# Splitting the time-step products of a Mamba-style scan into two fp16 parts

## The reference

```python
z, x, B_toks, C_toks, dt_toks = split(u @ W_in.T)     # 512, 512, 64, 64, 8
x, B_toks, C_toks = silu(causal_conv4(x, B_toks, C_toks))
A  = -exp(A_log)                                      # one value per head, 8 heads
dt = softplus(dt_toks + dt_bias)
dA = exp(dt * A)
# per token and head:
S = S * dA_t + outer(dt_t * x_t, B_t);  y_t = S @ C_t
y = (y + D * x) * silu(z);  out = y @ W_out.T
```

## Time and profile before

| | |
|---|---|
| median of 3 runs (lowest, highest) | 1589.3 us (1588.49, 1592.45) |
| profiled execution: span from first to last instruction | 1590.2 us (no other time is listed for it) |
| TensorE busy / VectorE / ScalarE / GpSimd | 1431.8 / 1034.1 / 592.3 / 541.7 us |
| mean granted TensorE clock | 0.962 of full |
| first stage / second stage | about 0 to 860 us / 860 to 1590 us |

### The profile page before, as it was taken

One profiled execution on the slowest core, in us unless ns is written; L12 is line 12 of the kernel. 1 busy time (PEld: TensorE's weight loads), 2 busy tenths in 40 slices (PEclk: granted clock), 3 DMA queues, 4 the chain that ended last, 5 costly groups with the idle time before them and its releaser, 6 DMA issues. The chain is left out here.

```text
span 1590.2 us, 23447 instructions
## 1 busy us (share of the span) xinstructions
PE 1431.8 (90%) x7392; PEld 707.9 (45%) x7392; DVE 1034.1 (65%) x2288; ACT 592.3 (37%) x1046; POOL 541.7 (34%) x653
## 2 busy tenths in 40 slices
PE   3798897898979988899886999999999999999998
PEld 1354443443535434445443444444444444444443
DVE  6799797897886978969885535435363545445333
ACT  4365554654645546555453221203020221213020
POOL 1275655556465555665754001010101001010101
PEclk9899998998999999989998999999999999999999
DMA  5011122022121221112201101010100101010000
GB/s 168 1 49 49 49 62 64 15 72 59 38 63 36 62 62 49 59 39 62 62 22 59 53 9 46 1 55 1 54 1 21 34 7 47 1 53 1 27 1 27
DMA packets 37454, 65.22 MB, mean 41 GB/s; under 512 B 5056, under 2 KB 15296, under 8 KB 37312
## 3 DMA queue, kind: packets, MB, share of 16 engines
q1 hardware_dynamic: 35424, 63.47, 12.7%
q10 hardware_dynamic: 1888, 0.03, 0.1%
HBM read 46.71 MB, written 16.78 MB: 40 GB/s over the span
## 5 line engine op out<-in xcount | busy, mean ns | idle before, releaser
L1386 ACT ACTIVATE gtanh<-bank,c_gate_half 128x512 f32<-128x512 f32 (+1 forms) x88 | 60.4, 687 | 537.0 <-PE bank L1421 537.0
L1421 PE MATMUL bank<-xt,ffn_hi 128*128 128x512 f16 (+1 forms) x704 | 213.8, 386 | 13.4 <-DVEq L82 6.7
L991 DVE TENSOR_SCALAR mask<-codes_h 128x416 f16<-128x416 f16 x640 | 215.5, 368 | 1.9
L1421 PE MATMUL bank<-xt_odd,ffn_hi 128*128 128x512 f16 (+1 forms) x704 | 209.4, 379 | 0.0
L1359 POOL TENSOR_TENSOR drstd<-dvar,neg_half 128x1 f32<-128x1 f32 x32 | 17.4, 545 | 481.1 <-DVE dvar L1518 481.1
L828 PE MATMUL bank<-mask,diag 128*128 128x416 f16 x640 | 133.2, 353 | 46.8 <-DVE mask L991 46.6
L1493 DVE SCALAR_TENSOR_TENSOR gsilu<-gtanh,bank 128x512 f32<-128x512 f32 (+1 forms) x88 | 60.5, 687 | 137.6 <-ACT gtanh L1386 137.4
L1421 PE MATMUL bank<-xt,ffn_lo 128*128 128x512 f16 (+1 forms) x352 | 135.7, 385 | 0.0
L1445 PE MATMUL bank<-ffn_hi,h_hi 128*128 128x512 f16 (+1 forms) x352 | 133.5, 379 | 0.0
L1421 PE MATMUL bank<-xt_odd,ffn_lo 128*128 128x512 f16 (+1 forms) x352 | 133.4, 379 | 0.0
L1445 PE MATMUL bank<-ffn_hi,h_lo 128*128 128x512 f16 (+1 forms) x352 | 133.3, 379 | 0.0
(11 more groups left out here) (184 smaller groups left out, 2768.3 us busy)
## 6 DMA issues: line engine op xcount, KB each, us to landing
codes_sb<-codes SPq DMA_DIRECT2D x80, 208.0 KB, 3.5
ut<-u SPq DMA_DIRECT2D x8, 1024.0 KB, 5.7
ures<-u SPq DMA_DIRECT2D x32, 256.0 KB, 2.7
x_scratch<-x SPq DMA_DIRECT2D x32, 256.0 KB, 2.0
xf<-x_scratch SPq DMA_DIRECT2D x8, 1024.0 KB, 5.9
out<-res SPq DMA_DIRECT2D x32, 256.0 KB, 2.0
ffn_hi<-w_in_t SPq DMA_DIRECT2D x4, 580.0 KB, 10.3
ffn_hi<-w_out_t SPq DMA_DIRECT2D x1, 1024.0 KB, 14.5
```

What stands on the lines that cost most here:

```text
L991: ins = nc.vector.tensor_scalar(mask[:, n, q, :], codes_h[:, n, :], float(2 * q), None, ALU.is_equal)
L1386: gtanh_ready.inc(nc.scalar.activation(gtanh[0:w, m % 2, :], banks[2 + m % 2][0:w, :], ACT.Tanh, scale=c_gate_half[0:w, :]))
L1421: last = nc.tensor.matmul(bank, wt[:, c0:c0 + w], xts[i][:, half, k, :], start=(k == 0 and n == 0), stop=(k == KC - 1 and n == 2))
```

## The change

Step 17 now writes dt * A * 2^7 in fp32 (`dax`); step 18 writes its high part in fp16 into `da[..., 0, :]`, clipped from below at -2^15; step 19 writes the remainder in fp16 into `da[..., 1, :]`; dt/4 becomes step 20. POOL's `segments` multiplies both parts, 2048 columns of fp16. The zero-one matrices get fp16 copies, made once on VectorE. TensorE adds the products of both parts in PSUM: four fp16 products of 512 columns, and six of 8 columns, for the chunk. The two exponentials take the scale 2^-7. In `time_steps` all 16 masks now stand beside steps 4 to 19.

```diff
-            da = st("da", [P, 2, SUB, HEADS])
+            dax = st("dax", [P, SUB, HEADS])
+            da = st("da", [P, 2, SUB, 2, HEADS], F16)
-            seg = st("seg", [P, HEADS, P])
+            seg = st("seg", [P, 2, HEADS, P], F16)
...
                         if c == 0:
-                            pool.wait_ge(dt_steps.sem, dt_steps.now(t, 17))
+                            pool.wait_ge(dt_steps.sem, dt_steps.now(t, 19))
                         seg_ready.inc(nc.gpsimd.tensor_tensor(
-                            seg[:], causal[:].unsqueeze(1).broadcast_to((P, HEADS, P)),
-                            da[:, p, c, :].unsqueeze(2).broadcast_to((P, HEADS, P)), ALU.mult))
+                            seg[:].rearrange("p n h t -> p (n h) t"),
+                            causal_h[:].unsqueeze(1).broadcast_to((P, 2 * HEADS, P)),
+                            da[:, p, c].rearrange("p n h -> p (n h)").unsqueeze(2).broadcast_to((P, 2 * HEADS, P)),
+                            ALU.mult))
...
-                        pe.wait_ge(dt_steps.sem, dt_steps.now(t, 17))
-                        for n, sums in enumerate((causal, below, ones)):
-                            last = nc.tensor.matmul(banks[3][:, 192 + n * HEADS:192 + (n + 1) * HEADS], sums[:],
-                                                    da[:, half, c, :], start=True, stop=True)
+                        pe.wait_ge(dt_steps.sem, dt_steps.now(t, 19))
+                        for n, sums in enumerate((causal_h, below_h, ones_h)):
+                            last = split_products(banks[3][:, 192 + n * HEADS:192 + (n + 1) * HEADS],
+                                                  [(sums[:], da[:, half, c, i, :]) for i in range(2)])
...
                         for n in range(2):
-                            last = nc.tensor.matmul(banks[4 + n][:], below[:],
-                                                    seg[:, 4 * n:4 * n + 4, :].rearrange("p h t -> p (h t)"),
-                                                    start=True, stop=True)
+                            last = split_products(banks[4 + n][:], [
+                                (below_h[:], seg[:, i, 4 * n:4 * n + 4, :].rearrange("p h t -> p (h t)"))
+                                for i in range(2)])
...
                         t_step(17, nc.vector.tensor_tensor(
-                            da[:, p], dt[:], a_sb[:].unsqueeze(1).broadcast_to((P, SUB, HEADS)), ALU.mult))
-                        t_step(18, nc.vector.tensor_scalar(dt4[:, p], dt[:], 0.25, None, ALU.mult))
+                            dax[:], dt[:], a_sb[:].unsqueeze(1).broadcast_to((P, SUB, HEADS)), ALU.mult))
+                        t_step(18, nc.vector.tensor_scalar(da[:, p, :, 0, :], dax[:], DA_LEAST * DAS, None, ALU.max))
+                        t_step(19, nc.vector.scalar_tensor_tensor(
+                            da[:, p, :, 1, :], dax[:], DA_LEAST * DAS, da[:, p, :, 0, :], ALU.max, ALU.subtract))
+                        t_step(20, nc.vector.tensor_scalar(dt4[:, p], dt[:], 0.25, None, ALU.mult))
...
-                            time_steps(i, p, lambda j: one_mask(row, half, 4, j))
-                            masks(row, half, 4, first=15)
+                            time_steps(i, p, lambda j: one_mask(row, half, 4, j) if j < 2 * PAIRS else None)
...
+                    for half, full in ((causal_h, causal), (below_h, below), (ones_h, ones)):
+                        nc.vector.tensor_copy(half[:], full[:]).then_inc(s_ident, 1)
```

More of the change, by code:

```diff
@@ L68 @@
 HSCALE = 2.0 ** -54
+DAS = 2.0 ** 7
+DA_LEAST = -2.0 ** 8
 class Signal:
@@ L161, in sandwich_kernel @@
         ident_h = sb("ident_h", [P, P], F16)
+        causal_h = sb("causal_h", [P, P], F16)
+        below_h = sb("below_h", [P, P], F16)
+        ones_h = sb("ones_h", [P, P], F16)
         dve_passed, pool_passed = sem("dve_waits_passed"), sem("pool_waits_passed")
@@ L272, in sandwich_kernel @@
             xs_ready = Signal(sem("conv_silu_ready"), FB + 1)
-            dt_steps = Signal(sem("dt_steps"), 18)
+            dt_steps = Signal(sem("dt_steps"), 20)
             dt_exp = Signal(sem("dt_exponential"), 1)
@@ L432, in weights @@
                         if c == 0:
-                            pool.wait_ge(dt_steps.sem, dt_steps.now(t, 18))
+                            pool.wait_ge(dt_steps.sem, dt_steps.now(t, 20))
                         xdt_ready.inc(nc.gpsimd.tensor_tensor(
@@ L541, in _ @@
                     front_rstd(0)
+                    pool.wait_ge(s_ident, 4)
                     pool.wait_ge(s_big, KC + 3)
@@ L642, in small @@
                         sums_ready.inc(nc.scalar.activation(
-                            ex[:], banks[3][:, 192:216].rearrange("p (k h) -> p k h", k=3), ACT.Exp))
+                            ex[:], banks[3][:, 192:216].rearrange("p (k h) -> p k h", k=3), ACT.Exp, scale=1.0 / DAS))
                         sums_ready.inc(nc.scalar.activation(bt[:], banks[3][:, 128:192], ACT.Copy))
@@ L649, in decays @@
                             decay_ready.inc(nc.scalar.activation(
-                                decay[:, 4 * n:4 * n + 4, :], banks[4 + n][:].rearrange("p (h t) -> p h t", h=4), ACT.Exp))
+                                decay[:, 4 * n:4 * n + 4, :], banks[4 + n][:].rearrange("p (h t) -> p h t", h=4), ACT.Exp, scale=1.0 / DAS))
                     def y_transposed(t, c):
@@ L952, in body @@
                         decode(t, 4, more)
-                    pe.wait_ge(s_ident, 1)
+                    pe.wait_ge(s_ident, 4)
                     for s in range(SUB):
@@ L1230, in _ @@
                     dve.wait_ge(s_alog, 1)
-                    step(nc.vector.tensor_scalar(a_sb[:], a_sb[:], -1.0, None, ALU.mult))
+                    step(nc.vector.tensor_scalar(a_sb[:], a_sb[:], -DAS, None, ALU.mult))
                     dt_input(0)
```

## The result

The changed kernel takes 1675.8 us (median of 5 runs, 1665.4 to 1677.2), the kernel before, run beside it, 1589.2: a ratio of 1.0531, 95% interval 1.0504 to 1.0557. It is slower by 86.6 us, four times the 20.8 that the sum gave, and outside the range. The profiled execution took 1665.4 us, with a span of 1663.7, so that what follows explains 73.5 us of the loss; the slower runs have no profile.

What follows compares the result with a forecast made beforehand. In the first stage TensorE and VectorE were taken to alternate, neither full, with VectorE stalled while POOL runs. Terms of +2.8 us a tile over 7 tiles (+19.6), +1.6 last tile, -0.4 front: +20.8, forecast 1610 us, range 1571 to 1625.

Steps and rivals of the forecast that it cites:

- Term 2: Chunk 1: seg(2) runs behind or ahead of VectorE's decay product, -1.3 or +2.3 us a tile; middle taken, +0.5.
- Terms 3 and 4: Chunks 2 and 3: mask beside seg(3) held longer, +1.3 us a tile; tile end up to prepare(0): about -0.1.
- Term 1: Chunk 0: longer seg(1) among unit 0's masks, +1.74 us, less 0.6 passed on from TensorE's savings: net +1.1 a tile.
- 9 us and more: Expected sign: the 16 masks of unit 0 take 9 us and more in place of 7.6.
- The last tile: Last tile, without time_steps and with few masks left: +1.6 us from the chunk 0 and chunk 1 terms.
- the front: Before the first tile: first seg holds VectorE, +2.2 us; prepare(0) at the low clock gives back 2.6: -0.4.
- TensorE's busy time: Expected sign: TensorE's busy time down by 40 to 50 us.
- By bytes: Rival: POOL's cost goes by bytes, seg stays at 1.91 us, -2.4 us a tile, 1570 us; chance 0.17.
- Falls into idle time: Rival: seg costs 3.65 us but VectorE's idle time absorbs it, -1.6 us a tile, 1577 us; chance 0.12.
- The two cancel: Rival: chunk 1 goes in VectorE's favour, +1.0 us a tile or less, within 0.3% (4.8 us); chance 0.12.
- Dearer still: Rival: by the skill page's rate each seg costs 0.85 us more, +2.5 a tile, 1628 us; chance 0.05.
- the case beside it: Near that rival: longer waits leave TensorE at its low clock for more of the stage; no size given.

Runs made afterwards that it cites:

- pe_twice: Changed kernel with each pair of segment products issued twice and each pair of chunk sums four times, results the same: 1636.2 us, ratio 1.0260.
- warm: Changed kernel with 14 more TensorE products of 512 columns, never read, between the two input transposes of chunk 1: 1646.3 us, ratio 1.0342.
- short03: Changed kernel with seg(3) and seg(0) cut to 1024 columns (high part only), seg(1) and seg(2) long: 1634.5 us, ratio 1.0272.
- masks_first: Kernel before with unit 4's first mask ahead of the time steps, the other 15 beside them, dt/4 ahead of da: 1578.8 us, ratio 0.9924.
- half_seg: Changed kernel with every seg cut to its high part, 1024 fp16 columns, which each segment product uses twice: 1606.4 us, ratio 1.0102.
- two_ops: Changed kernel with seg written by two POOL instructions of 1024 columns in place of one of 2048: 1636.7 us, ratio 1.0272.
- half_gates: Changed kernel with seg cut to its high part and two more POOL waits for VectorE's decay products of chunks 0 and 1: 1589.8 us, ratio 0.9978.

## Why the prediction was wrong

The direction was right: seg at 3.62 us (forecast 3.65), the sums and segment products at 0.16 and 0.86 us (0.15 and 0.87), dt/4 stalled for 3.6. It was the sum over the path that failed, in three terms.

- **Term 2, chunk 1, is the step that failed**: +0.5, with bounds of -1.3 and +2.3, against +5.3 (mean over tiles). I had weighed two orders, the decay product ahead of seg(2) or behind it, and taken the middle. TensorE's saving moved z gate 2 and seg(2) ahead in all eight tiles; with the saving undone four fall back (pe_twice). In six tiles the case that I had weighed came, the decay product held (4.31 us), and the bound was too low for it: these tiles lost 1.2 to 7.5 us in chunk 1, 4.9 in the mean, since the bound had neither TensorE's clock in it nor, for three of them, a late seg(1). In the other two the second input split was held, and they lost 6.4 and 6.9: I had left it out, though the splits stand ahead of the decay product in VectorE's queue, and TensorE's transposes of them ahead of the scan. warm says how much goes through the clock: 16 us by the profiled executions, 30 by the medians, of 86.
- **Terms 3 and 4, the tile end**: +1.3 and -0.1, against -0.5 from `prepare(2)` to `prepare(3)` and +3.6 from there on. From the first instruction of unit 4's masks to the end of cs VectorE takes 1.9 us longer, as forecast (13.9 to 15.8). But it came to that point 4.0 us later behind `prepare(3)` (33.3 to 37.3 us), and the slack before `prepare(0)` was 2.7: 4.0 + 1.9 - 2.7 = 3.2, which is what this tile lost (49.93 to 53.12). For term 3 I had counted 1.7 less 0.4; two rows of VectorE show 1.7 for the mask beside seg(3), with no slack behind it, and 1.5 for conv(0), which now lies beside POOL's residual add:

```profile
573.86 3.55 DVE L1001 TENSOR_SCALAR mask<-codes_h 128x416 f16<-128x416 f16 x1
...
584.31 3.87 DVE L1029 SCALAR_TENSOR_TENSOR cacc<-cin,conv_w_sb,cacc 128x512 f32<-128x512 f32 x3
```

  Short segs there give back 3.6 us a tile (short03). The order of the masks was right by itself (masks_first).
- **Term 1, chunk 0**: +1.1 forecast, +1.2 measured, for a reason I didn't give. It is the mean of five tiles that lost 1.7 to 3.6 us and three that gained 1.1 to 2.0. In the fifth tile the masks grew by 0.8, not 1.7, and started later, as POOL's first state decay got ahead of them. "9 us and more" for the masks came in three tiles of eight, and their mean did not grow (7.0 us), so the number is right by luck.
- **The last tile** lost 4.8 us, not 1.6, in the same places; the front lost 1.9 in place of gaining 0.4.
- **TensorE's busy time** fell by 8 us, not 40 to 50: the low clock stretched what remained.

The rivals. *By bytes* fell with the duration of seg, and its time was wrong too: with seg at 1.91 us the kernel takes 1606 (half_seg), where I had 1570, since I took a saving of TensorE for a gain whenever nothing got longer. *Falls into idle time* fell: the gap after the decay product is there only as long as POOL reaches it after VectorE. *The two cancel* didn't come, and its sum was wrong too: +1.0 us a tile is 7 us over seven tiles, more than the 4.8 within which it was to lie. *Dearer still* had its price wrong, but the case beside it, TensorE at its low clock for more of the stage, is what happened. I gave it no price of its own, and the rows had one: the segment products at 3.53 us at the low level.

The Trainium skill (SBUF — State Buffer, "Who interferes with whom") says of the pair of ports that VectorE and GpSimd share: "it's an exclusive lock", held for the whole instruction by whichever starts first. The trace agrees: 5.54 us for the pair of splits beside seg(2), whose second outlasts seg(2) by 0.5 us, and 3.82 once seg was two instructions; seg(2) itself, which came while a split was under way, took 4.05 us and not 3.60. The rule prices a long POOL instruction by what it may meet, in either order, and not by its share of busy time. The rate that the prediction took from the Trainium skill (GPSIMD Engine Reference, "Elementwise — side-by-side cycle accounting", 4.50 us for 2048 columns of fp32) did not hold for this fp16 product: 3.62.

What stays open: the profiled execution of the changed kernel is 10 us below its median, and nothing here says where the slower runs lose the rest (their mean granted clock is 0.936 to 0.939, against 0.940). What decides in a tile whether seg(1) comes before or behind the masks I did not follow. Nor was a changed kernel tried that has both parts of seg and TensorE's saving and is faster than before; the nearest, two_ops, is at 1.027.

## What to carry to other kernels

Where two engines can't run side by side, a longer instruction costs what it meets, so ask for each of them which instruction of the other engine it will lie beside once everything around it has moved, and follow the queue from there; split the long one, or put it where the other engine runs what it doesn't disturb. A saving on an engine that waits was no gain here (half_gates), and it can do harm, as it sends the work behind it out early. Look at all the tiles before you name the instruction that pays: the one read first was the exception here. And price a new wait of TensorE twice, for its length and for the stretch at the low clock behind it.

## What the runs showed of the hardware

- A POOL product of two operands, both of them broadcast along one axis, costs 1.91 us for 1024 columns and 3.62 for 2048 in fp16, and 1.91 for 1024 in fp32: fp16 gains nothing there. In one kernel (short03), both lengths:

```profile
L430 POOL TENSOR_TENSOR seg<-causal_h,da x32: 1892/2766/4050, 52.5 to 877.2; 128x1024 f16<-128x1024 f16 x16, 128x2048 f16<-128x2048 f16 x16
```

- I had not expected filler work to pay: 3 us of products a tile that nobody reads made the kernel 30 us faster by the medians (16 by the profiled executions), with a mean granted clock of 0.88 in place of 0.72 in the part of the tile where they lie.
- VectorE's stalls and POOL's are mutual: POOL is busy for 68.6 us more (610.3 against 541.7), of which seg itself makes 55 (119.1 against 63.6); the other 13 lie in its other operations, and a seg(2) beside the splits took 4.05 where 3.60 is the least.
